# Causal mask of an attention on VectorE (PSUM to SBUF) in place of TensorE's mask products, with the outputs' low halves moved ahead

## The reference

```python
Q1, Q2 = jnp.split(Q, 2, axis=-1)          # 16 heads, 2 x 32 channels each
K1, K2 = jnp.split(K, 2, axis=-1)
causal = jnp.tril(jnp.ones((n, n), bool))
A1 = jnp.where(causal, jnp.einsum('bhnd,bhmd->bhnm', Q1, K1) * scaling, -jnp.inf)
A2 = jnp.where(causal, jnp.einsum('bhnd,bhmd->bhnm', Q2, K2) * scaling, -jnp.inf)
attn = jax.nn.softmax(A1, axis=-1) - lam * jax.nn.softmax(A2, axis=-1)
O = jnp.einsum('bhnm,bhmd->bhnd', attn, V)
rms = jnp.sqrt(jnp.mean(O * O, axis=-1, keepdims=True) + EPS)
O = O / rms * rms_scale * (1.0 - LAMBDA_INIT)
return O.transpose(0, 2, 1, 3).reshape(b, n, H * 2 * dh) @ Wo.T
```

## Time and profile before

| | |
|---|---|
| median of 3 runs | 1761.76 us (1761.65 to 1762.83) |
| profiled execution, own time | 1760.7 us |
| its span | 1758.9 us |
| self attention in it | some 1343 to 1551 us |
| busy in the span | TensorE 95%, VectorE 67%, ScalarE 53%, GpSimd 37% |

### The profile page before, as it was taken

How to read it: one execution, slowest core, us unless ns; L and a number is a source line. 1 busy time by engine, 2 the same in 40 slices (tenths; PEclk the granted TensorE clock), 3 DMA queues, 4 the chain that set the end, 5 groups by cost and what they waited for, 6 DMA issues and landing times. The chain is left out here.

```text
span 1758.9 us, 37626 instructions
## 1 busy us (share of the span) xinstructions
PE 1671.9 (95%) x16090; PEld 1370.0 (78%) x16090; DVE 1172.6 (67%) x1554; ACT 935.0 (53%) x1406; POOL 649.9 (37%) x352
## 2 busy tenths in 40 slices
PE   7999999999999999999999999677998899889999
PEld 6788888888888888888888888566886677658886
DVE  5137787887878788788878878787434666652223
ACT  4237666666666666666666666662104776520000
POOL 0004555555555555555555555002000433522220
PEclk9999999999999999999999999878999999999998
DMA  5210111101111010111101100213422111111101
GB/s 191 65 50 27 40 42 30 40 30 42 31 38 43 29 40 30 42 35 34 44 28 40 30 30 5 77 51 105 162 90 85 49 49 49 49 49 48 48 0 48
DMA packets 73088, 88.61 MB, mean 50 GB/s; under 512 B 6746, under 2 KB 39514, under 8 KB 72930
## 3 DMA queue, kind: packets, MB, share of 16 engines
q1 hardware_dynamic: 72930, 86.31, 15.7%
HBM read 71.62 MB, written 14.68 MB: 49 GB/s over the span
## 5 line engine op out<-in xcount | busy, mean ns | idle before, releaser
L633 POOL TENSOR_TENSOR b_acc<-b_acc,b_s 128x1024 f32<-128x1024 f32 x168 | 459.1, 2733 | 258.1 <-ACT b_s L841 247.5
L870 DVE TENSOR_TENSOR b_s<-b_s,b_mb 128x2048 f32<-128x2048 f32 x128 | 365.3, 2855 | 3.9 <-ACT b_mb L824 3.9
L908 DVE TENSOR_TENSOR b_mx<-b_psS,b_mx 128x512 f32<-128x512 f32 x480 | 331.1, 690 | 52.3 <-PE b_psS L705 39.1
L841 ACT ACTIVATE b_s<-b_s 128x2048 f32<-128x2048 f32 x128 | 245.2, 1916 | 81.6 <-DVE b_s L870 81.6
L850 ACT ACTIVATE b_s<-b_psS 128x2048 f32<-128x2048 f32 x128 | 241.0, 1883 | 69.8 <-DVE b_mx L908 69.8
L43 PE MATMUL b_work<-wvT,cT 128*128 128x512 f32 x496 | 203.0, 409 | 0.0
L43 PE MATMUL b_work<-cT,wkT 128*128 128x512 f32 x496 | 200.2, 404 | 0.0
L45 PE MATMUL b_work<-wvT,cT 128*128 128x512 f32 x496 | 194.2, 392 | 0.0
L45 PE MATMUL b_work<-cT,wkT 128*128 128x512 f32 x496 | 193.7, 390 | 0.0
L44 PE MATMUL b_work<-wvT,cT 128*128 128x512 f32 x496 | 193.5, 390 | 0.0
L44 PE MATMUL b_work<-cT,wkT 128*128 128x512 f32 x496 | 193.5, 390 | 0.0
(11 more groups left out here) (250 smaller groups left out, 2891.5 us busy)
## 6 DMA issues: line engine op xcount, KB each, us to landing
cin<-in_ctx SPq DMA_DIRECT2D x64, 512.0 KB, 3.8
experts_sb<-in_L_ffn_expert_w SPq DMA_DIRECT2D x8, 1024.0 KB, 5.8
q_scratch<-d_st SPq DMA_DIRECT2D x16, 256.0 KB, 2.3
k_scratch<-d_st SPq DMA_DIRECT2D x16, 256.0 KB, 2.3
e_q<-q_scratch SPq DMA_DIRECT2D x16, 256.0 KB, 2.7
k_sb<-k_scratch SPq DMA_DIRECT2D x16, 256.0 KB, 2.9
b_kT<-in_x SPq DMA_DIRECT2D x4, 512.0 KB, 8.1
q_scratch<-a_q SPq DMA_DIRECT2D x8, 256.0 KB, 2.3
```

What stands on the lines that cost most here:

```text
L633: nc.gpsimd.tensor_tensor(acc[:, :, :], acc[:, :, :], s[:, buf, 2 * i:2 * i + 2, :], ALU.add).then_inc(sum_done, 1)
L841: nc.scalar.activation(part, part, ACT.Exp, scale=SCALE).then_inc(exp_done, 1)
L870: nc.vector.tensor_tensor(s[:, n % BUFS, :, :], s[:, n % BUFS, :, :], mb[:, :].rearrange("p (o n) -> p o n", o=1).broadcast_to([P, CHUNK, ...
L908: nc.vector.tensor_tensor(mx[:, :, :], part, mx[:, :, :], ALU.max).then_inc(mx_done, 1)
```

## The change

The mask products on TensorE and the identity in bfloat16 are gone. Each score product is now a sum of its own (`start` and `stop` both true). VectorE adds the mask, from `psS` in PSUM into the buffer `sm` of the maps in SBUF: maps 0 and 1 in an instruction each, maps 2 and 3 in one. The minima are taken from `sm`, and the exponentials are made in place in `sm`. `psS` is free when the three additions are done, and no longer when the exponentials are. The wait for the transposes that free `sm` goes from ScalarE to VectorE. Lo goes from its place behind the minima of maps 2 and 3 to the head of a half, ahead of the x add.

```diff
         def _(pe):
-            def masks(b, hf, maps):
-                for j in maps:
-
-                    reached(pe, exp_done, b * 8 + (4 * hf + j - 3))
-                    nc.tensor.matmul(psS[:, j, :, :], ident_b[:, :], mask_b[:, :, :], start=True, stop=False)
-
             def scores(b, hf):
                 pe.wait_ge(qk_in[hf], b * 32 + 32)
+
+                reached(pe, masked, b * 6 + 3 * hf)
                 for u in range(N):
                     for j in range(HG):
                         rows = slice(j * HD, (j + 1) * HD)
                         last = nc.tensor.matmul(psS[:, j, u, :], q2[rows, hf, u, :], k2[rows, hf, u, :],
-                                                start=False, stop=u == N - 1)
+                                                start=True, stop=True)
...
-                    if front:
-                        masks(b, hf, (0, 1))
...
-                        masks(b, hf, (2, 3))
                         scores(b, hf)
...
                             act.wait_ge(low_done, b * 6 + (3 * hf + min(j, 2) + 1))
-                            if j % 2 == 0:
-
-                                reached(act, a_full, b * 4 + (2 * hf + i - 3))
                             for u in range(N):
-                                last = nc.scalar.activation(sm[:, hf, i, j % 2, u, :], psS[:, j, u, :], ACT.Exp,
+                                last = nc.scalar.activation(sm[:, hf, i, j % 2, u, :], sm[:, hf, i, j % 2, u, :], ACT.Exp,
...
-            def lowest(hf, maps):
-                nc.vector.tensor_reduce(low[:, hf, maps, :], psS[:, maps, :, :], AX.X, ALU.min).then_inc(low_done, 1)
+            def mask(b, hf, m0, m1):
+
+                reached(dve, a_full, b * 4 + (2 * hf + m0 // 2 - 3))
+                nc.vector.tensor_tensor(maps_of(hf)[:, m0:m1, :, :], psS[:, m0:m1, :, :],
+                                        mask_b[:, :, :].rearrange("p (o u) k -> p o u k", o=1)
+                                        .broadcast_to([P, m1 - m0, N, P]), ALU.add).then_inc(masked, 1)
+
+            def lowest(b, hf, m0, m1):
+                dve.wait_ge(masked, b * 6 + (3 * hf + min(m0, 2) + 1))
+                nc.vector.tensor_reduce(low[:, hf, m0:m1, :], maps_of(hf)[:, m0:m1, :, :], AX.X,
+                                        ALU.min).then_inc(low_done, 1)
...
                 for hf in range(2):
+                    if end if hf == 0 else out:
+
+                        p = 1 - hf
+                        dve.wait_ge(w_hi, b * 2 + (hf - 4))
+                        nc.vector.scalar_tensor_tensor(
...
                         dve.wait_ge(s_full, b * 2 + (hf + 1))
-                        lowest(hf, slice(0, 1))
-                        lowest(hf, slice(1, 2))
+                        mask(b, hf, 0, 1)
+                        mask(b, hf, 1, 2)
+                        lowest(b, hf, 0, 1)
+                        lowest(b, hf, 1, 2)
...
-                        lowest(hf, slice(2, 4))
-                    if end if hf == 0 else out:
-
-                        p = 1 - hf
-                        dve.wait_ge(w_hi, b * 2 + (hf - 4))
...
+                        mask(b, hf, 2, 4)
+                        lowest(b, hf, 2, 4)
```

More of the change, by code:

```diff
@@ L935, in __init__ @@
         self.mask_b = sb("e_mask_b", [P, HG, P], BF16)
-        self.ident_b = sb("e_ident_b", [P, P], BF16)
         self.qk_in = [ctx.enter_context(nc.semaphore(f"e_qk_in{i}")) for i in range(2)]
@@ L1111, in _ @@
             dve.wait_ge(made, 2)
-            nc.vector.tensor_copy(consts.ident_b[:, :], ident[:, :])
             nc.vector.tensor_copy(consts.mask_b[:, :, :], mask[:, :].rearrange("p (o n) -> p o n", o=1)
@@ L1290, in differential_attention @@
         coef, rs, expo, three = consts.coef, consts.rs, consts.expo, consts.three
-        mask_b, ident_b, qk_in = consts.mask_b, consts.ident_b, consts.qk_in
+        mask_b, qk_in = consts.mask_b, consts.qk_in
         k2, q2, woT, sm, o_sb, sq, on, oT = (bufs.k2, bufs.q2, bufs.woT, bufs.sm, bufs.o_sb, bufs.sq,
@@ L1313, in differential_attention @@
         s_full = sem("e_s_full")
+        masked = sem("e_masked")
         low_done = sem("e_low_done")
@@ L1577, in _, with maps_of @@
         def _(dve):
-            def lowest(hf, maps):
-                nc.vector.tensor_reduce(low[:, hf, maps, :], psS[:, maps, :, :], AX.X, ALU.min).then_inc(low_done, 1)
+            def mask(b, hf, m0, m1):
[7 more added lines that the diff above has]
+                                        ALU.min).then_inc(low_done, 1)
+            def maps_of(hf):
+                return sm[:, hf, :, :, :, :].rearrange("p i s u k -> p (i s) u k")
             def weigh(b, hf, at, i):
@@ L1601, in batch @@
                 for hf in range(2):
+                    if end if hf == 0 else out:
+                        p = 1 - hf
+                        dve.wait_ge(w_hi, b * 2 + (hf - 4))
+                        nc.vector.scalar_tensor_tensor(
+                            out=oT[1][:, 4 * p:4 * p + 4, :].rearrange("p k t -> p (k t)"), in0=psO[p][:, :],
+                            scalar=rs[:, 0:1], in1=f32(oT[0][:, 4 * p:4 * p + 4, :]).rearrange("p k t -> p (k t)"),
+                            op0=ALU.mult, op1=ALU.subtract).then_inc(w_lo, 1)
                     if end and hf == 1:
```

## The result

The change made the kernel slower: 1784.72 us (median of 4 runs, 1782.95 to 1784.91) against 1762.3 us before (1761.65 to 1763.13) on the same chip, a ratio of 1.0127 with a 95% interval of 1.0113 to 1.0141. The prediction had 1771.5, with a range from 1762 to 1780: the side was right, the size was not.

What follows compares the result with a forecast made beforehand. The prediction took TensorE to bound batches 3 to 7 before, and a chain through Lo at VectorE's head to rule after. Steps 6.3, exponentials 0.8 and clock 3 made +10 us: 1771.5 us, range 1762 to 1780.

Steps and rivals of the forecast that it cites:

- TensorE's clock: New wait ahead of T1 may bring the low clock: between 0 and eight times 1.5, taken as 3 us.
- the clock in every batch: Slower rival: low clock 8 x 1.5, exponentials fully exposed, GpSimd slowing minima from SBUF; 1782 us, chance 0.18.
- The chain: T0 through ScalarE's Wh to Lo at VectorE's head, x add and additions queued behind: steps 12.67 and 12.31 us.
- the sum: Steps of batches 2 to 7 and the part behind the last scores: 1.1 + 3.0 + 3.1 - 0.9 = +6.3 us.
- batches 0 and 1, taken as nothing: No Lo there: masks lost (0.97 a half) against 1.2 of added path; no change, 2 us either way.
- The exponentials: ScalarE reading SBUF: 33 ns more each, eight in six first halves make 1.6 us if exposed; 0.8 taken.
- The tail: Behind the last scores T1 comes 0.4 later, two projections that waited for Lo save 0.65 each: less 0.9 us.
- TensorE stays the bound: Faster rival: TensorE's saving counts in full, 3.9 x 5 = 20 us less, 1743 us; chance 2 in 100.
- Lo doesn't hold: Faster rival: the scores, not Lo, decide when additions start; steps 11.34 and 11.33 us, about 1755 us; chance 0.10.

Runs made afterwards that it cites:

- the filling: Changed kernel plus products of 128x512 whose result nobody reads, issued ahead of T1 while TensorE would wait; with every long wait filled 1774.27 us.
- Lo mid: Kernel before with Lo moved ahead of the minima of maps 2 and 3, behind W1: 1754.12 us; with three waits filled 1753.61 us.
- run with PSUM and full clock: Changed kernel with masked scores written back into PSUM, minima and exponentials read there, and unread products filling all long waits of T1: 1775.91 us.
- the change with Lo mid: Changed kernel with Lo moved from the head to ahead of the addition of maps 2 and 3, behind W1: 1764.25 us, ratio 1.0011.

## Why the prediction was wrong in size

**The step that failed is "TensorE's clock"**: "I take three of 1.0, 3 us, as the waits are shorter than 2.92". The traces show the low clock in the first halves of batches 1 to 6, six of them, and in the four steady ones it costs 2.1 us each (14.6 less 12.5), which the filling gave back. In batches 1 and 2 it costs 0.64 (11.40 against 10.76) and 0.66 (12.57 against 11.91). Together 9.7 us where I had 3; the difference of the two walks, 9.64, agrees. Not all of it is new: the kernel before has a low stretch in batch 1 too, and filling its wait took 0.9 us off that step (9.43 to 8.57 with Lo mid). Both factors were too small. The count: I took a wait of 2.5 to be mostly harmless because one of 2.92 had once been so. The price: I took it from the O of the earlier trace rows, 2.70 us, which had run at 1.2 GHz only in part; a whole one takes 3.51. The granted clock was 0.50 for 3.4 us there (1370.93 to 1374.35), for 6.8 us in each first half of batches 3 to 6 of the change (1475.30 to 1482.13 in batch 5), and the projection and T0 are slow as well: the copy of T0 starts 11.60 behind m (1481.48) where it starts 9.57 behind it at full clock. The rival that I gave 18 in 100, the clock in every batch, is what came closest, with 8 x 1.5 = 12 for the clock and 1782 in all. Of its other part, minima from SBUF slowed by GpSimd, nothing came: two of them took 1.27 us, from PSUM 1.29.

**What the miss is made of.** The forecast was +10.1 us and the two profiled spans differ by 23.9. Of the 13.8 between, some 6.6 are the clock, 1.9 the steps at full clock, 2.6 the tail, 1.7 the experts' stage and 0.9 the first m, which comes at another time in every trace. With the right clock the forecast would have been 1778, inside its range.

**The chain** held by its own steps. Lo at the head waits for Wh and holds x add and additions; W1 is done at +4.0 and T1 starts at +4.03 (predicted 4.05); T1 waits 2.32 (2.5); T0 at +9.54 in a second half (9.66), +8.15 in a first at full clock (8.24); a step from second to first half 12.55 (12.67). The walk at full clock is 9.9 us over before where the sum says 8.0 (6.3, without the tail's -0.9 that is 7.2, and 0.8). What is missing is batches 0 and 1, taken as nothing "2 us either way": they cost 2.1. Lo is not there yet, and the kernel with masks on TensorE and Lo at the head takes what before does in them, so it is the masks on VectorE that cost it. "At full clock" leaves out batch 0, whose first waits nothing filled: the granted clock is 0.50 there for 6.8 us before (from 1350.45) and for 10.2 after (from 1349.01).

**The exponentials** from SBUF start 42 ns further apart, not 33 as the long ones, and all eight are exposed: 0.34 in each of the first halves of 12.50. The run with PSUM and full clock gave 0.24 of it back. The Trainium skill, VectorE: DVE Perf Modes, on the TRN2 errata, would make it 43 ns each, an estimate from its cycles, and this trace agrees; the 0.8 in the middle was too low, the 1.6 of eight times 33 as well.

**The tail** was to save 0.9 and costs 1.7 to the last x add. Behind the last m, T1 starts 4.02 later where it started 2.84 later before (I had counted 0.4), and the first x add comes 1.5 later. Two projections that waited 1.01 and 1.00 for Lo now wait 0.44, for the x add (0.57 saved each of the 0.65 forecast), but the one between them waits 1.64 instead of 0.25; I had not looked at it. Filling the last long wait shortened nothing there (36.6 from the last m to the last x add, against 36.0), so TensorE's clock is not what makes the tail long.

**The faster rivals.** "TensorE stays the bound" came true in no run with the masks on VectorE; with masks left on it and Lo mid it does, at 11.04 a step and some 7 us under before, since only the wait of O goes. "Lo doesn't hold" is what the change with Lo mid does, and one of its two steps is the rival's 11.34; the other takes 11.9, since T0 waits 0.35 for W0, which stands behind Lo there, and it ends at 1764, not 1755.

What stays open: why the same wait of 2.32 is followed by 1.2 GHz in batches 3 to 6 and not in batch 7 (O 1.90, step 12.50). The fall came a little later from batch to batch, 1.24, 1.29, 1.39 and 1.60 us behind the start of T1 (1419.45 and 1420.69 in batch 3), and in the run with the masked scores back in PSUM batch 7 had it too. Open as well are 1.7 us of the experts' stage. From the last x add to the end it takes 208.5 before and 210.2 after, but 210.3 with masks on TensorE and Lo mid and 208.7 with masks on VectorE and Lo in its old place, so it doesn't follow the masks.

## What to carry to other kernels

When work leaves the bounding engine, don't only ask which chain takes over: look at how long the relieved engine now waits in one piece, because the low clock that can follow has a price of its own. An instruction that waits at the head of an in-order queue costs what is queued behind it: against the place in the middle, Lo at the head cost 4 us in front of minima alone and 20 in front of additions and minima, 13 of these with every long wait filled and the rest by the clock; try its place by itself before moving work to another engine. And a low stretch in one place may depend on what ran batches before: count such stretches over the whole trace, and fill all the waits or none.

## What the runs showed of the hardware

- Waits of TensorE of 2.3 us, shorter than the 2.92 of before, were followed by a granted clock of 0.50 in four batches of five (in all five with the masked scores in PSUM, no filling), and so were two waits of 1.1 and 2.1 us with transposes between them, while single waits of 1.11 us never were (nine halves in the kernel with Lo mid).
- The clock can be held by products that nobody needs: nine of 128x512 (2.20 us) in a wait of 2.3 us kept O at 1.90 us and made the kernel faster.
- Filling one wait moved the fall to the next batch, behind a wait of 2.9 us that had been harmless without it, and cost 4.1 us there for 0.9 gained.
- At 1.2 GHz the products of 128x512 start 0.43 us apart instead of 0.23, and O's sixteen take 3.51 instead of 1.90.
- Minima from SBUF take what they take from PSUM (1.27 against 1.29 for two); exponentials of 128 columns don't (0.385 against 0.343 start to start).
